# Deformable sampling, a scan and a mixture of experts in one kernel: a running sum over experts, interpolation on column groups, and half of the corner sum on GpSimd

## Chip, cores and metric

One core of a Trainium2 chip runs the program. The time is the device time of one execution in microseconds (us); three executions of the kernel before took 2467.89, 2460.09 and 2467.79, with a median of 2467.79 us.

## What is computed

For each of 16 images (64 channels, 128 x 128 pixels): bilinear samples of the image on a 32 x 32 grid give 1024 queries; a small network makes 8 sampling points of each query; bilinear samples there (four corners each) give keys and values; attention over the 8 points, with 8 heads, gives 1024 tokens. With 128 text tokens these 1152 tokens pass a linear recurrence over the batch and a mixture of 16 experts, of which each token uses two. Cut to what matters here:

```python
q_feat = bilinear_sample(feature_map, ref[:, :, None, :])[:, :, 0]
queries = q_feat @ W_q.T
h = jax.nn.gelu(layer_norm(q_feat @ W_o1 + b_o1, ln_g, ln_b))
off = (h @ W_o2 + b_o2).reshape(B, Nq, NHEAD, 2) * OFFSET_SCALE
sampled = bilinear_sample(feature_map, ref[:, :, None, :] + off * scale)
# bilinear_sample: v00*(1-wx)*(1-wy) + v01*wx*(1-wy) + v10*(1-wx)*wy + v11*wx*wy
...
hidden = jax.nn.silu(x @ w1[e]) * (x @ w2[e])        # for each of 16 experts e
out = sum over e of dispatch[:, e] * (hidden @ w3[e])  # dispatch is zero but for two experts
h = h + out
```

All of it is in float32.

## The kernel before

**Stages.** The kernel works through 16 images ("batches", index b). Per batch:

- `A1` (16 pieces): TensorE (PE) transposes the image from the load buffer `xin` (L712), ScalarE copies it to `pixmaj`, pixel rows with 64 channels (L843). SP stores `pixmaj` as a table in device memory.
- `A2` (8 pieces): PE interpolates the 32 x 32 grid, each of its 32 grid rows from two pixel rows (L727). The pixel row is the stationary operand (128 x 64), the interpolation matrix (32 columns) the moving one. ScalarE copies the result, 64 channels by 1024 queries, to `qfT` in two halves (L850).
- `B0`, `B1`: queries and the first layer of the offset network, 8 matmuls each (L735, L741), contraction over 64 partitions. `B1` to `B6` go on to the indices `idx` (L1142) and the corner weights `cw`. GpSimd takes the inverse square root in `B1` as a power (L585).
- `G` (32 pieces): GpSimd issues 64 gathers of 128 rows (L570), two a piece. Each row holds four corners. Behind each piece it clears a small tile `rest` (L577), `RESTS` = 2 times, waiting for each clearing to end.
- `D1` (j, f; 16 pieces): VectorE multiplies 512 KB of gathered rows by the corner weights into the one buffer `wsam` (L1062). `D2`: PE transposes the weighted rows and adds the four corners in PSUM as it does, 2 pairs x 4 corners (L690). ScalarE copies to `samT`; `D3`: PE computes keys and values (L700), ScalarE copies, VectorE multiplies by the query (L1068). `D5`, `S1` to `S3`: scores, softmax and the weighted sum of values on VectorE (L1072 to L1101).
- For each of three groups g of 384 tokens, `P1` to `P8`: layer norms (GpSimd takes their inverse square roots, L590), the recurrence, the gate, and the two best experts, which give `disp` (L1052).
- `X` (g, e; 48 pieces): PE computes both hidden products of one expert in three rotating banks `bank_h` (L624, L625); ScalarE applies silu (L780); VectorE multiplies into `hid` (L967), which holds all 16 experts.
- `W` (g, half, k; 18 pieces): for 128 tokens and 8 experts, PE multiplies `hid` (stationary, 128 x 128) by `w3` (moving, 64 columns) into `bank_o` (L634). ScalarE scales the eight results by `disp` in eight instructions (L831). `Z` on VectorE halves them in three additions (L975, L976) and `M2` adds both halves and the residual (L984, L985). SP stores the group.

A float32 matmul shows as two passes in the trace, each a weight load (PEld) and a product (PE); a transpose as one.

**What sets the order.** Nothing is scheduled when the program runs. For each engine's queue a string `ORDER` names the pieces in the order in which that engine does them, and every engine does its queue strictly in order. PE holds the pieces of three neighbouring batches interleaved with the experts: in the middle of the run PE's 48 `X` of a batch are mostly one or two pieces apart. `X(n)` waits for `hid(n-2)` and the silu of `n-1`, because it rewrites their banks. `W` waits for eight `hid`, and for the scaling of the last use of its bank. `D1` waits for its gathers and for the `D2` before (one `wsam`); a gather piece waits for the `D1` that last read its buffer (two buffers of 8 gathers). GpSimd's queue holds, per batch, 32 `G`, the power steps `P1`, `P5` (three each) and `B1`.

## Time and profile before

| | value |
|---|---|
| median of three runs | 2467.79 us |
| the profiled execution's own time | 2476.72 us |
| its span | 2474.9 us |
| PE busy | 2210.1 us, 89% |
| PE weight loads busy | 1979.4 us, 80% |
| VectorE busy | 1856.8 us, 75% |
| ScalarE busy | 1399.1 us, 57% |
| GpSimd busy | 1673.7 us, 68% |
| granted PE clock, mean share of full speed | 0.943 |

PE has the most work, and in the chain of waits that ended last it holds 58%, VectorE 11%, ScalarE 10%, GpSimd 8%, and 11% is "issue", time in which an engine waited for nothing that the profile shows. The shares are averages over a start in which the first image has to come in, a long middle in which one batch is like the next, and an end with experts only. Issuing instructions count as idle, so for GpSimd, which issues the gathers, the busy share leaves work out.

### The profile page before, as it was taken

The page shows a single profiled execution, that of the slowest core. Times are in us where ns is not written, and L with a number is a line of the kernel's source. Part 1 is how long each engine was busy: PE and PEld are TensorE (multiplying, and loading weights), DVE is VectorE, ACT ScalarE, POOL GpSimd, SP SyncE. Part 2 cuts the span into 40 slices and gives each one's busy share as a digit, 9 for nine tenths or more (in the row PEclk, how much of TensorE's full clock was granted, in tenths as well). Part 3 has the DMA queues.
Part 4 walks back from the last instruction along what each step waited for, and adds up shares of the span by engine and source line. Part 5 has one row for each costly group of instructions (what it writes and reads, how often), then busy time and mean ns, then how long its engine had stood idle before and what let it go on. Part 6 is the DMA issues. An engine that isn't in the chain of part 4 may idle for free.

```text
span 2474.9 us, 46859 instructions
## 1 busy us (share of the span) xinstructions
PE 2210.1 (89%) x15441; PEld 1979.4 (80%) x15441; DVE 1856.8 (75%) x4865; ACT 1399.1 (57%) x4344; POOL 1673.7 (68%) x2168
## 2 busy tenths in 40 slices
PE   2578989989999998999999899999999999989887
PEld 1566778888888888879889888888889888878776
DVE  1226888788788778888787878878787888887765
ACT  1124466566665656566565656656565666655555
POOL 0378887777686858868586877858686786867500
PEclk9967999999999999999899999989999999989989
DMA  9575636356472736538272745638173563712100
GB/s 221 148 207 154 182 104 186 113 164 173 110 217 66 213 97 177 167 106 222 77 212 85 198 138 152 186 95 225 52 221 108 166 175 109 201 52 68 49 3 6
DMA packets 362993, 346.85 MB, mean 140 GB/s; under 512 B 49152, under 2 KB 313472, under 8 KB 362624
## 3 DMA queue, kind: packets, MB, share of 16 engines
q1 hardware_dynamic: 313600, 209.57, 31.4%
q0 software_dynamic: 49152, 134.28, 18.6%
q8 instruction: 124, 2.03, 0.3%
q14 instruction: 117, 0.96, 0.1%
HBM read 205.87 MB, written 137.89 MB: 139 GB/s over the span
## 4 chain that ended last, share of the span: by engine, by line
PE 58%; issue 11%; DVE 11%; ACT 10%; POOL 8%; DMA 2%; ACTq 0%; DVEq 0%; another core or an unknown queue 0%; POOLq 0%
PE bank_o L634 16%; PE bank_h L624 8%; PE bank_d L700 7%; PE bank_h L625 7%; PE bank_d L690 7%; POOL gath L570 5%; ACT scaled L831 5%; PE bank_a L727 5%; PE bank_a L712 2%; POOL rest L577 2%; DMA gath<-table,idx 2%; DVE hid L967 2%; DVE wsam L1062 1%; PE bank_p L655 1%; PE bank_a L741 1%
## 5 line engine op out<-in xcount | busy, mean ns | idle before, releaser
L570 POOL DMA_INDIRECT gath<-table,idx x1024 | 1110.6, 1085 | 267.2 <-issue 238.5
L831 ACT ACTIVATE scaled<-bank_o,disp 128x64 f32<-128x64 f32 x2304 | 502.2, 330 | 370.8 <-PE bank_o L634 334.4
L624 PE MATMUL bank_h<-xsplit,w 128*128 128x384 f32 x1536 | 634.7, 413 | 83.3 <-ACT silu L780 52.9
L634 PEld LDWEIGHTS bank_o<-w_sb,hid 128*128 128x128 f32 x4608 | 567.9, 197 | 10.1 <-DVE hid L967 9.6
L634 PE MATMUL bank_o<-w_sb,hid 128*128 128x64 f32 x4608 | 563.8, 278 | 6.3 <-DVE hid L967 6.2
L625 PE MATMUL bank_h<-xsplit,w 128*128 128x384 f32 x1536 | 539.0, 351 | 0.0
L780 ACT ACTIVATE silu<-bank_h 128x384 f32<-128x384 f32 x768 | 393.8, 514 | 122.0 <-PE bank_h L625 104.2
L967 DVE TENSOR_TENSOR hid<-silu,bank_h 128x384 f32<-128x384 f32 x768 | 416.8, 548 | 53.4 <-ACT silu L780 38.5
L577 POOL MEMSET rest<- 1x400 f32 x1024 | 432.1, 422 | 29.6
L624 PEld LDWEIGHTS bank_h<-xsplit,w 128*128 128x128 f32 x1536 | 307.6, 200 | 139.5 <-ACT silu L780 68.0
L1062 DVE TENSOR_TENSOR wsam<-gath,cw 128x1024 f32<-128x1024 f32 x256 | 312.6, 1221 | 115.4 <-PE bank_d L690 54.7
L975 DVE TENSOR_TENSOR scaled<-scaled 128x256 f32<-128x256 f32 x576 | 205.8, 357 | 198.8 <-ACT scaled L831 165.5
L590 POOL TENSOR_TENSOR lns<-lns,neghalf 128x3 f32<-128x3 f32 x96 | 105.4, 1097 | 333.1 <-DVE lns L944 332.3
L690 PE MATMUL bank_d<-eye,wsam 128*128 128x128 f32 x2048 | 288.7, 287 | 37.5 <-DVE wsam L1062 33.2
L700 PE MATMUL bank_d<-w_kv,samT 128*128 128x256 f32 x1024 | 289.1, 406 | 29.9 <-ACT v_sb L817 17.4
L625 PEld LDWEIGHTS bank_h<-xsplit,w 128*128 128x128 f32 x1536 | 309.1, 201 | 4.7
L690 PEld LDWEIGHTS bank_d<-eye,wsam 128*128 128x128 f32 x2048 | 244.0, 149 | 55.8 <-DVE wsam L1062 44.1
L712 PE MATMUL bank_a<-eye,xin 128*128 128x128 f32 x1024 | 186.0, 312 | 80.4 <-DMA xin<-x_dram 39.0
L700 PEld LDWEIGHTS bank_d<-w_kv,samT 128*128 128x128 f32 x1024 | 183.4, 196 | 73.8 <-issue 39.3
L843 ACT COPY pixmaj<-bank_a 128x512 f32<-128x512 f32 x256 | 152.9, 597 | 154.8 <-PE bank_a L712 140.6
L712 PEld LDWEIGHTS bank_a<-eye,xin 128*128 128x128 f32 x1024 | 140.1, 161 | 116.6 <-issue 60.1
L813 ACT COPY k_sb<-bank_d 128x256 f32<-128x256 f32 x256 | 97.9, 382 | 166.9 <-PE bank_d L700 145.3
(141 smaller groups left out, 2306.2 us busy)
## 6 DMA issues: line engine op xcount, KB each, us to landing
table<-pixmaj SPq DMA_DIRECT2D x80, 1024.0 KB
xin<-x_dram SPq DMA_DIRECT2D x256, 256.0 KB
table<-pixmaj SPq DMA_DIRECT2D x32, 960.0 KB
table<-pixmaj SPq DMA_DIRECT2D x16, 1088.0 KB
gath<-table,idx POOLq DMA_INDIRECT x1024
out_dram<-ob SPq DMA_DIRECT2D x48, 96.0 KB
gath<-w_dram SPq DMA_DIRECT2D x4, 512.0 KB, 8.8
interp_sb<-interp_dram SPq DMA_DIRECT2D x1, 1024.0 KB, 5.3
```

The source lines that it names most:

```text
L570: pool.indirect_dma_start(out=gath[buf][:, p, :, :].rearrange("p a c -> p (a c)"), out_offset=None, in_=table[par], in_offset=bass.Indirec ...
L577: nc.gpsimd.memset(rest[:], 0.0).then_inc(rested, 1)
L624: mm(bank[:, 0:GC], w12[:, e, which, 0, :], xsplit[gp][:], start=True, stop=False)
L625: mm(bank[:, 0:GC], w12[:, e, which, 1, :], xsplit[gp][:], start=False, stop=True).then_inc(ready, 1)
L634: last = mm(bank_o[n % 2][:, C * i:C * (i + 1)], hid[:, e, 128 * k:128 * (k + 1)], w3_sb[:, e, :], start=True, stop=True)
L690: last = mm(bank_d[:, 128 * (2 * f + pair):128 * (2 * f + pair + 1)], wsam[:, corner, 2 * pair:2 * pair + 2, :].rearrange("p n c -> p (n c)"),
L700: last = mm(bank_d[:, 256 * i:256 * (i + 1)], samT[:, 2 * f + i, :], w_kv[:], start=True, stop=True)
L712: last = mm(bank_a[:, 128 * r:128 * (r + 1)], xin[u % 2][:, HW * (4 * (c % 2) + r):HW * (4 * (c % 2) + r + 1)], eye[:], start=True, stop=T ...
L780: nc.scalar.activation(silu[e % 2][:], bank_h[r][:, 0:GC], ACT.Silu).then_inc(silu_done, 1)
L831: last = nc.scalar.activation(scaled[n % 2][:, i, :], bank_o[n % 2][:, C * i:C * (i + 1)], ACT.Identity, scale=disp[gpar(par, g)][:, k, e: ...
L967: tt(hid[:, e, :], silu[e % 2][:], bank_h[r][:, 0:GC], ALU.mult).then_inc(hid_done, 1)
L1062: tt(wsam[:].rearrange("p a n c -> p n a c"), gath[j % GB][:, 4 * f:4 * f + 4, :, :], spread(w, 3, C), ALU.mult).then_inc(weighted, 1)
```

## The change

- The sum over experts becomes a running sum. `W` is now a piece per expert (48 a batch): three matmuls, one for each 128 tokens. ScalarE's part is gone. `Z` is now a piece per expert: three instructions of VectorE (scalar_tensor_tensor, 128 x 64) read `bank_o`, multiply by the token's `disp` and add the running sum in `ob`; the first expert adds the residual `h2` instead. Each waits for the one on the same tokens of the expert before. `M2`'s additions, `scaled` and `part` are gone. `hid` holds 4 experts (`HB`) for 16.
- The interpolation runs on column groups. The interpolation matrix (128 x 32) is now stationary, at one of four column positions, and the pixel row (64 columns) moves. The result stands with queries on partitions; a new piece `A3` transposes it (4 transposes, one more copy by ScalarE in place of one of the two). `B0` and `B1` now take two blocks of queries in one matmul, with block-diagonal weights `w_blk`: 4 matmuls each for 8.
- The corners are summed in two steps. A new piece `F` on GpSimd, two for each half `f` of a `j` (32 a batch), adds the far two corners to the near two (128 x 256 each); `D2` then has 2 pairs x 2 corners. `wsam` has two buffers. `RESTS` is 1.
- `ORDER` is new for every engine. `W(e)` stands behind `X(e+2)` on PE, `Z(e)` behind `hid(e+2)` on VectorE. On GpSimd the `F` pieces stand between the `G` pieces.

One batch of GpSimd's new queue, the middle one, read from the diff (G with its number, F with j, f and pair):

```
G0 G1 G2 G3 G4 G5 G6 P1 G7 F000 F001 F010 F011 G8 F100 G9 F101 G10 F110 G11 F111
P5 G12 F200 G13 F201 G14 F210 G15 F211 G16 F300 G17 F301 G18 P1 F310 G19 F311 G20
F400 F401 G21 F410 F411 G22 P5 F500 G23 F501 G24 G25 F510 G26 F511 G27 F600 G28
F601 G29 P1 F610 G30 F611 G31 B1 F700 F701 F710 F711 P5
```

The diff, without the order strings and the bookkeeping of semaphores:

```diff
-RESTS = 2
+RESTS = 1
+HB = 4
...
-        w_q = sb("w_q", [C, C])
-        w_off1 = sb("w_off1", [C, LH])
+        w_blk = sb("w_blk", [128, 2 * C + 2 * LH])
...
-        qfT = sb("qfT", [C, NQ])
+        qf_sb = sb("qf_sb", [128, QT * C])
+        qfT = sb("qfT", [128, QT // 2, 128])
...
-        wsam = sb("wsam", [128, 4, 4, C])
+        wsam = [sb(f"wsam{i}", [128, 4, 4, C]) for i in range(2)]
...
-        hid = sb("hid", [128, NE, GC])
-        scaled = [sb(f"scaled{i}", [128, 8, C]) for i in range(2)]
-        part = sb("part", [128, 2, GT, C])
+        hid = sb("hid", [128, HB, GC])
...
+        block_loads += [(w_blk[C * p:C * (p + 1), C * p:C * (p + 1)], wq) for p in range(2)]
+        block_loads += [(w_blk[C * p:C * (p + 1), 2 * C + LH * p:2 * C + LH * (p + 1)], w_o1) for p in range(2)]
...
-                wait(sp, ob_done, NGRP * b + g + 1)
+                wait(sp, eo_added, GT * NE * (NGRP * b + g + 1))
...
+                    elif kind == "F":
+                        j, f, pair = args
+                        pool.wait_ge(weighted, 16 * b + 2 * j + f + 1)
+                        near = wsam[f][:, 0:2, 2 * pair:2 * pair + 2, :].rearrange("p a n c -> p a (n c)")
+                        far = wsam[f][:, 2:4, 2 * pair:2 * pair + 2, :].rearrange("p a n c -> p a (n c)")
+                        nc.gpsimd.tensor_tensor(near, near, far, ALU.add).then_inc(folded, 1)
...
                     elif kind == "W":
-                        g, half, k = args
-                        n = 2 * GT * (NGRP * b + g) + GT * half + k
-                        pe.wait_ge(hid_done, SLOTS * b + NE * g + 8 * half + 8)
-                        wait(pe, eo_scaled, n - 1)
-                        for i in range(8):
-                            e = 8 * half + i
-                            last = mm(bank_o[n % 2][:, C * i:C * (i + 1)], hid[:, e, 128 * k:128 * (k + 1)],
+                        g, e = args
+                        n = SLOTS * b + NE * g + e
+                        pe.wait_ge(hid_done, n + 1)
+                        wait(pe, eo_added, GT * (n - 1))
+                        for k in range(GT):
+                            last = mm(bank_o[n % 2][:, C * k:C * (k + 1)], hid[:, n % HB, 128 * k:128 * (k + 1)],
                                       w3_sb[:, e, :], start=True, stop=True)
...
-                        pe.wait_ge(weighted, 16 * b + 2 * j + f + 1)
+                        pe.wait_ge(folded, 2 * (16 * b + 2 * j + f + 1))
...
-                            for corner in range(4):
+                            for corner in range(2):
 
                                 last = mm(bank_d[:, 128 * (2 * f + pair):128 * (2 * f + pair + 1)],
-                                          wsam[:, corner, 2 * pair:2 * pair + 2, :].rearrange("p n c -> p (n c)"),
-                                          eye[:], start=corner == 0, stop=corner == 3, is_transpose=True)
+                                          wsam[f][:, corner, 2 * pair:2 * pair + 2, :].rearrange("p n c -> p (n c)"),
+                                          eye[:], start=corner == 0, stop=corner == 1, is_transpose=True)
...
-                        if n == 4:
-                            pe.wait_ge(qf_stored, 2 * b + 1)
-                        for i in range(4 * n, 4 * n + 4):
-                            for r in range(2):
-                                row = FIRST_ROW[i] + r
-                                last = mm(bank_a[0:C, NG1 * (i % 16):NG1 * (i % 16 + 1)],
-                                          pixmaj[:, C * row:C * (row + 1)], interp_sb[:, i, r, :],
-                                          start=r == 0, stop=r == 1)
-                        if n % 4 == 3:
+                        for r in range(2):
+                            for a in range(4):
+                                row = FIRST_ROW[4 * n + a] + r
+                                last = mm(bank_a[NG1 * a:NG1 * (a + 1), C * n:C * (n + 1)], interp_sb[:, 4 * n + a, r, :],
+                                          pixmaj[:, C * row:C * (row + 1)], start=r == 0, stop=r == 1,
+                                          tile_position=(0, NG1 * a))
+                        if n == 7:
                             last.then_inc(qf_ready, 1)
+                    elif kind == "A3":
+                        pe.wait_ge(qf_stored, b + 1)
+                        for m in range(QT // 2):
+                            last = mm(bank_a[:, 128 * m:128 * (m + 1)], qf_sb[:, 128 * m:128 * (m + 1)], eye[:],
+                                      start=True, stop=True, is_transpose=True)
+                        last.then_inc(qfT_ready, 1)
...
                     elif kind == "B0":
-                        pe.wait_ge(qf_stored, 2 * b + 2)
-                        for t in range(QT):
-                            last = mm(bank_a[:, C * t:C * (t + 1)], qfT[:, 128 * t:128 * (t + 1)], w_q[:],
+                        pe.wait_ge(qfT_stored, b + 1)
+                        for m in range(QT // 2):
+                            last = mm(bank_a[:, 128 * m:128 * (m + 1)], qfT[:, m, :], w_blk[:, 0:2 * C],
                                       start=True, stop=True)
                         last.then_inc(q_ready, 1)
                     elif kind == "B1":
                         pe.wait_ge(q_stored, b + 1)
-                        for t in range(QT):
-                            last = mm(bank_a[:, LH * t:LH * (t + 1)], qfT[:, 128 * t:128 * (t + 1)], w_off1[:],
+                        for m in range(QT // 2):
+                            last = mm(bank_a[:, 2 * LH * m:2 * LH * (m + 1)], qfT[:, m, :], w_blk[:, 2 * C:2 * C + 2 * LH],
...
-                    elif kind == "W":
-                        g, half, k = args
-                        n = 2 * GT * (NGRP * b + g) + GT * half + k
-                        act.wait_ge(eo_ready, n + 1)
-                        act.wait_ge(disp_done, NGRP * b + g + 1)
-                        wait(act, pair_sum, n - 1)
-                        for i in range(8):
-                            e = 8 * half + i
-                            last = nc.scalar.activation(scaled[n % 2][:, i, :], bank_o[n % 2][:, C * i:C * (i + 1)],
-                                                        ACT.Identity, scale=disp[gpar(par, g)][:, k, e:e + 1])
-                        last.then_inc(eo_scaled, 1)
...
-                    elif kind == "A2" and args[0] % 4 == 3:
-                        half = args[0] // 4
-                        if half == 0 and b == 0:
+                    elif kind == "A2":
+                        if b == 0:
                             setup()
-                        act.wait_ge(qf_ready, 2 * b + half + 1)
+                        act.wait_ge(qf_ready, b + 1)
+                        wait(act, qfT_ready, b)
+                        copy(qf_sb[:], bank_a[:]).then_inc(qf_stored, 1)
+                    elif kind == "A3":
+                        act.wait_ge(qfT_ready, b + 1)
                         wait(act, off1_ready, b)
-                        copy(qfT[:, 512 * half:512 * (half + 1)], bank_a[0:C, :]).then_inc(qf_stored, 1)
+                        copy(qfT[:].rearrange("p a b -> p (a b)"), bank_a[:]).then_inc(qfT_stored, 1)
...
-                        if e % 8 == 0:
-
-                            wait(dve, eo_ready, 2 * GT * (NGRP * b + g - 1) + GT * (e // 8 + 1))
+                        wait(dve, eo_ready, n - HB + 1)
                         r = (2 * (NE * g + e) + 1) % 3
-                        tt(hid[:, e, :], silu[e % 2][:], bank_h[r][:, 0:GC], ALU.mult).then_inc(hid_done, 1)
+                        tt(hid[:, n % HB, :], silu[e % 2][:], bank_h[r][:, 0:GC], ALU.mult).then_inc(hid_done, 1)
                     elif kind == "Z":
-                        g, half, k = args
-                        n = 2 * GT * (NGRP * b + g) + GT * half + k
-                        sums.start(n)
-                        dve.wait_ge(eo_scaled, n + 1)
-                        eo = scaled[n % 2]
-                        for m in (4, 2):
-                            link(sums, tt(eo[:, 0:m, :], eo[:, 0:m, :], eo[:, m:2 * m, :], ALU.add))
-                        tt(part[:, half, k, :], eo[:, 0, :], eo[:, 1, :], ALU.add).then_inc(pair_sum, 1)
-                    elif kind == "M2":
-                        g = args[0]
+                        g, e = args
                         gp = gpar(par, g)
-                        mix.start(NGRP * b + g)
-                        dve.wait_ge(pair_sum, 2 * GT * (NGRP * b + g + 1))
-
-                        wait(dve, out_done[gp], 8 * NGRP * b + 8 * (g - gp))
-                        link(mix, tt(ob[gp][:], part[:, 0, :, :], part[:, 1, :, :], ALU.add))
-                        tt(ob[gp][:], ob[gp][:], h2[g][:], ALU.add).then_inc(ob_done, 1)
+                        n = SLOTS * b + NE * g + e
+                        dve.wait_ge(eo_ready, n + 1)
+                        if e == 0:
+                            wait(dve, out_done[gp], 8 * NGRP * b + 8 * (g - gp))
+                        for k in range(GT):
+                            if e:
+                                dve.wait_ge(eo_added, GT * (n - 1) + k + 1)
+                            stt(ob[gp][:, k, :], bank_o[n % 2][:, C * k:C * (k + 1)], disp[gp][:, k, e:e + 1],
+                                (ob[gp] if e else h2[g])[:, k, :], ALU.mult, ALU.add).then_inc(eo_added, 1)
...
-                        wait(dve, sam_ready, 16 * b + 2 * j + f)
+                        wait(dve, sam_ready, 16 * b + 2 * j + f - 1)
                         w = cw[par][:, HEADS * j + 4 * f:HEADS * j + 4 * f + 4, :]
-                        tt(wsam[:].rearrange("p a n c -> p n a c"), gath[j % GB][:, 4 * f:4 * f + 4, :, :],
+                        tt(wsam[f][:].rearrange("p a n c -> p n a c"), gath[j % GB][:, 4 * f:4 * f + 4, :, :],
```

## Rows read from the trace of the kernel before

**Rows 1.** The window 500 to 2000 us: length; busy (x) of PE, PEld, DVE, ACT, POOL; PEclk, DMA, GB/s
```profile
500.00:2000.00 1500.00, 1409.12 (x10117) 1275.29 (x10117) 1213.53 (x3186) 921.27 (x2871) 1112.13 (x1434) 0.96 0.55 152
```

**Rows 2.** Timeline, VectorE: `idx` (L1142) of batches 3 and 15, start and duration
```profile
499.45 0.23 DVE L1142 SCALAR_TENSOR_TENSOR idx<-xyf 128x64 int32<-128x64 f32 x1
...
2203.99 0.23 DVE L1142 SCALAR_TENSOR_TENSOR idx<-xyf 128x64 int32<-128x64 f32 x1
```

**Rows 3.** What POOL waits for in 500 to 2000 us: total, times, longest
```profile
POOL lns L590 <- DVE lns L944: 186.2, 37, 17.7
POOL gath L570 <- issue: 158.0, 669, 0.4
```

**Rows 4.** ScalarE and VectorE groups of the expert sum, whole run: busy, mean ns, idle before
```profile
L831 ACT ACTIVATE scaled<-bank_o,disp 128x64 f32<-128x64 f32 x2304 | 502.2, 330 | 370.8 <-PE bank_o L634 334.4
...
L975 DVE TENSOR_TENSOR scaled<-scaled 128x256 f32<-128x256 f32 x288 | 121.6, 422 | 188.9 <-ACT scaled L831 165.5 <-issue 19.4 <-DVE disp L1052 2.8
L975 DVE TENSOR_TENSOR scaled<-scaled 128x128 f32<-128x128 f32 x288 | 84.2, 292 | 9.9
L976 DVE TENSOR_TENSOR part<-scaled 128x64 f32<-128x64 f32 x288 | 65.0, 226 | 9.8
```

**Rows 5.** Timeline, VectorE: one piece `Z`, then two small steps of `P8`
```profile
1306.21 0.74 DVE L975 TENSOR_TENSOR scaled<-scaled 128x256 f32<-128x256 f32 x2
1306.98 0.22 DVE L976 TENSOR_TENSOR part<-scaled 128x64 f32<-128x64 f32 x1
1307.13 0.55 DVE L967 TENSOR_TENSOR hid<-silu,bank_h 128x384 f32<-128x384 f32 x1
...
1316.93 0.21 DVE L1050 TENSOR_TENSOR disp<-disp,top_p 128x48 f32<-128x48 f32 x1
1317.06 0.20 DVE L1051 TENSOR_TENSOR pick<-pick,top_p 128x48 f32<-128x48 f32 x1
```

**Rows 6.** Window 500 to 2000 us, PE and PEld busy: L690, L727, L735, L741 in order
```profile
500.00:2000.00 1500.00, 182.26 (x1344) 155.37 (x1344) 0.96 0.55 152
500.00:2000.00 1500.00, 87.98 (x1280) 80.19 (x1280) 0.96 0.55 152
500.00:2000.00 1500.00, 19.95 (x160) 18.57 (x160) 0.96 0.55 152
500.00:2000.00 1500.00, 20.31 (x160) 19.31 (x160) 0.96 0.55 152
```

**Rows 7.** Chain of waits from 1301 us: start, duration, engine and line
```profile
1301.52 0.17 PE bank_h L624
1301.86 1.73 PE bank_o L634 x16
1303.59 0.23 PE bank_h L624
...
1309.55 0.88 PE bank_d L690 x8
```

**Rows 8.** GpSimd groups by shape in 500 to 2000 us, then a setup clearing
```profile
L570 POOL DMA_INDIRECT gath<-table,idx x681 | 739.5, 1086 | 176.6 <-issue 158.0 <-DVE idx L1142 18.4 <-DVE wsam L1062 0.2
L577 POOL MEMSET rest<- 1x400 f32 x680 | 287.0, 422 | 19.6
L590 POOL TENSOR_TENSOR lns<-lns,neghalf 128x3 f32<-128x3 f32 x63 | 71.0, 1127 | 186.7 <-DVE lns L944 186.2
...
L554 POOL MEMSET w_kv<- 128x256 f32 x1 | 0.3, 316 | 0.0
```

**Rows 9.** Timeline: a gather beside a two-input VectorE instruction; durations (min/median/max) of all gathers
```profile
1434.02 2.23 DVE L1090 TENSOR_TENSOR v_sb<-v_sb,score 128x2048 f32<-128x2048 f32 x1
1434.36 2.72 POOL L570 DMA_INDIRECT gath<-table,idx  x1 [0.30 <-issue]
...
L570 POOL DMA_INDIRECT gath<-table,idx x1024: 942/959/3055, 102.6 to 2329.4; - x171
```

**Rows 10.** Groups, whole run: the passes of `W`, busy and mean duration
```profile
L634 PE MATMUL bank_o<-w_sb,hid 128*128 128x64 f32 x4608 | 563.8, 278 | 6.3 <-DVE hid L967 6.2
```

205 lines of the change are left out of this document (108 added, 97 removed), and 8 rows, old and new, of the table KINDS.

## Prediction

> **What bounds the kernel now.** I read the busy table first, then a long stretch in the middle, because one batch is repeated 16 times and only the first three and the last run differently. From 500 to 2000 us PE is busy 1409 of 1500 us, VectorE 1214, GpSimd 1112, ScalarE 921 [rows 1]. The indices of batch 3 are ready at 499.45 us and those of batch 15 at 2203.99 us [rows 2], so a batch takes 1704.5 / 12 = 142.05 us. Multiplying row 1 by 142.05 / 1500 = 0.0947 gives the work of one batch: PE 133.4, VectorE 114.9, ScalarE 87.2, GpSimd 105.3 us. PE is idle for 8.6 us of a batch, and it is the bound.
>
> The reader should not stop at GpSimd's 105.3. Between its gathers the profile shows 158.0 us of "issue", 15.0 a batch, that is not counted as busy and can hold nothing else [rows 3]. GpSimd's own work is therefore 120.3 us a batch; what is left is mostly waiting for layer norm variances (186.2 us in the window, 17.6 a batch). So three engines stand at 133, 120 and 115 of 142. A change that takes work from PE and gives some to the other two can gain only until the next of them is full.
>
> **The expert sum.** ScalarE loses its 2304 scalings, 502.2 us of the run, 31.4 a batch [rows 4]. It was not the bound; the gain is that a silu no longer queues behind eight of them. VectorE loses 18 pieces `Z` a batch. One lasts from 1306.21 to the next start at 1307.13, 0.92 us [rows 5]: 16.6 us. It also loses `M2`: two additions of 192 columns, which by the slope between 128 and 256 columns (292 and 422 ns, 1.02 ns a column [rows 4]) are 0.36 us each, three times a batch: 2.1 us. It gains 48 x 3 = 144 multiply-adds of 64 columns. Neither a 64-column step on PSUM with a scalar per partition nor its spacing is in the trace. Below: two steps of 48 columns that don't depend on each other start 0.13 us apart [rows 5]. Above: if each must end before the next, it is 226 ns [rows 4] plus the 0.03 us gap of the dependent steps in `Z` [rows 5], 0.256. Each of the 144 waits on the sum three instructions back, never on its neighbour, so I take the near end with 16 more columns, rounded up: 0.16 us, 23.0 us a batch (18.7 to 36.9). VectorE: 114.9 - 16.6 - 2.1 + 23.0 = 119.2.
>
> PE keeps the same 288 passes a batch of `W` (144 matmuls, two passes each), but in 48 pieces for 18. The first step of an `X` holds the chain 0.23 us behind a `W` and 0.17 behind another `X` [rows 7]: 30 x 0.06 = +1.8 us. `W(e)` stands behind `X(e+2)` in the new order, whose own wait already asks for `hid(e)`, so it adds no wait of its own for that. It also waits for `Z(e-2)`, which VectorE does right behind `hid(e)`, 0.48 us later, while `X(e+2)` holds PE for 0.7 (four steps of 0.17 [rows 7]); hidden, unless other VectorE work lies between. `hid(n)` needs `W(n-4)`, long past. SP's output now waits for the last `Z`; its store stands at no one's head.
>
> **Corners.** `D2` goes from 128 transposes a batch to 64. Removed are 64 passes: 0.110 us each in the chain (0.88 / 8 [rows 7]) or 0.136 by busy time (182.26 / 1344 [rows 6]), so 7.0 to 8.7; I take 8.0. The second `wsam` lets `D1` start earlier, worth nothing while VectorE isn't the bound.
>
> **Interpolation.** `B0` and `B1` were 160 passes each in the window, 19.95 and 20.31 us [rows 6], 3.8 a batch, and are halved: -1.9. The new `A3` is four transposes: +0.45. `A2` keeps 128 passes, 87.98 us or 8.3 a batch, 0.065 each [rows 6]. Its weights shrink from 64 to 32 columns and its moving side grows from 32 to 64. Below: half of now, 4.2, if the weights set the pace and the four column groups run together. Above: a pass of `W` with the same 64 moving columns under 128 columns of weights, 1.73 / 16 = 0.108 [rows 7], 13.8. I stay near the present kind, at 7.3: -1.0. Where the row shows one `W` pass lasting 278 ns at a spacing of 108 [rows 7, 10], an emptied array would cost 0.17 us more; the new order has 103 runs of `A2`, 12.9 changes of form a batch, 2.2 us.
> The Trainium skill, TensorEngine Tiling (Array Packing), Key Properties, says that changing the tiling mode drains TensorE. By that rule those 2.2 us would be added to PE's sum; no row of before has a tiled matmul.
>
> PE: 133.4 + 1.8 - 8.0 - 1.9 + 0.45 - 1.0 = 124.8 us. With its present 8.6 of idle time it would allow 133.4 a batch.
>
> **GpSimd.** One clearing of two goes: 0.422 us and 0.029 of gap (19.6 / 680) [rows 8], 32 x 0.451 = -14.4. In its place 32 additions of two 256-column operands. Below: a clearing of 256 columns, 0.316 us, which reads nothing. Above: the power step, 1.127 us on 3 columns [rows 8], a heavier function. An add is nearer the clearing in kind but moves three streams for one, so I take twice it: 0.65.
> The Trainium skill, GPSIMD Engine Reference, Performance versus the Vector engine, gives 4497 ns for such an add of 2048 elements; an eighth is 0.56, an estimate, and with it the forecast would be some 35 us lower.
>
> That is not all. The gather that starts at 1434.36 lasts 2.72 us, to within a microsecond of the end of a 2.23 us VectorE instruction that reads two SBUF operands; the shortest takes 0.942 [rows 9], the mean 1.086 [rows 8]. So a GpSimd instruction loses 0.14 us on average to VectorE. I give each addition 0.15: 0.80 in all, 25.6 a batch. The same collision may hold two-input VectorE steps, for which no row has a price: from nothing to the whole of every addition, 32 x 0.65 = 21 us. If VectorE lost per addition what a gather loses, it would be 4.6; GpSimd lost rather than shared in that row, so I take about half, 2.5: VectorE 121.7.
>
> GpSimd: 120.3 - 14.4 + 25.6 = 131.5 us, now the fullest. Moved into its in-order queue are waits: each `F` waits for `D1`, and the later gathers and the power steps wait behind it. The order issues two to three gather pieces (4 to 6 gathers) after the last one that an `F` needs, but one at `F(5,0)` and none at `F(7,1)`; the latter stands where GpSimd waits for indices anyway. For this I add 6 us, less than PE's 8.6 because GpSimd has those gathers in hand: 137.5 us a batch.
>
> **The sum.** 12 batches x (137.5 - 142.05) = -55. The first batches follow GpSimd alone: +32 x 0.35 = +11. After the last index PE and ScalarE set the pace with fewer steps: -9. Together -53 on the profiled execution's own 2476.7 us: 2424. That execution was 8.9 above the median of the runs, so I predict 2415 us.
>
> **Rivals.**
> (B) The addition is cheap. At 0.316 + 0.15 GpSimd needs 120.8 and PE is again the bound at 133.4: 12 x -8.7 = -104, +1, -12, so 2353. For it: nothing in the trace shows an arithmetic GpSimd step without the power function.
> (C) GpSimd's queue becomes a bound worse than PE is now. It decides on F, the addition with what holds it, at its place behind each `D1`: 120.3 - 14.4 + 32 F + 6 passes 142.05 at F = 0.94 us. At 1.0 it is 143.9 a batch: +22, +18, -8, so 2500; with the power step's price far above. For it: the 2.72 us gather. Against: the clearing's 0.316.
> Ours lies between B and C, on one number. The Trainium skill, SBUF — State Buffer, SBUF: two separate sides, says the shared pair of ports is locked for a whole instruction and the loser fully blocks. The trace agrees with its 2.72 us gather; what a reading GpSimd step does to VectorE no row of before shows.
> (D) The running sum is serial: 0.256 a step makes VectorE 135.6, with its waits about 144.3 a batch, 2495. Against: the waits reach three steps back.
> (E) The column groups give nothing and drain the array: `A2` at 13.8 and 2.2 more put PE at 133.5, with 8.6 idle 142: 2465, no change. This is the tiling rule at full price.
>
> **Numbers.** Ours 0.47, B 0.22, C 0.19, D 0.04, E 0.08. About 0.3% is what a measurement of this kernel tells from no change. Faster is ours and B less the edge of ours, 0.68; the same 0.09; slower 0.23. The range takes in B's end and C's first step: 2340 to 2500.
>
> **What would show it.** The addition's mean near 0.8 us with VectorE steps beside the long ones; GpSimd busy near 120 a batch with little left but issue; L634 unchanged in passes, L690 halved; multiply-adds 0.16 apart; a period of 137 to 138. An addition over 0.94 or a period set by waits of GpSimd for `wsam` makes it wrong upwards; one near 0.4 with PE at 94% again, downwards.

## The result, and the profile after

The changed kernel takes 2514.46 us, the median of 4 runs (2511.19 to 2525.84). Four runs of the kernel before beside it gave 2466.61. The ratio is 1.0208, with a 95% interval of 1.0171 to 1.0245: slower by 48 us, where 2415 us had been forecast, and outside the range of 2340 to 2500. The profiled execution took 2514.73 us. One kernel further down, the kernel before with one clearing, had two of its four runs in a slower state (2839.01 and 3242.29 us), so beside its median of 2828.59 stand its two fast runs, 2790.00 and 2818.18 us.

The busy table of the page:

```profile
PE 2068.7 (82%) x14225; PEld 1826.0 (73%) x14225; DVE 2167.8 (86%) x6209; ACT 955.1 (38%) x2040; POOL 1871.3 (74%) x2169
```

The window from 500 to 2000 us, with the columns of [rows 1]:

```profile
500.00:2000.00 1500.00, 1284.64 (x9080) 1144.40 (x9079) 1380.68 (x3972) 611.12 (x1305) 1201.63 (x1379) 0.92 0.52 147
```

VectorE's timeline has the indices of batches 3 and 15, as in [rows 2]:

```profile
508.04 0.22 DVE L1146 SCALAR_TENSOR_TENSOR idx<-xyf 128x64 int32<-128x64 f32 x1
...
2269.28 0.22 DVE L1146 SCALAR_TENSOR_TENSOR idx<-xyf 128x64 int32<-128x64 f32 x1
```

A batch takes 1761.2 / 12 = 146.8 us, where it took 142.05. The spans differ by 38.0 us: +8.6 up to batch 3, +56.7 in the twelve periods, -27.3 after the last indices. The window times 146.8 / 1500 gives PE 125.7 us a batch, VectorE 135.1, ScalarE 59.8 and GpSimd 117.6. PE's granted clock is 0.92 there for 0.96, but PE is idle for 21 us of a batch. All that GpSimd waits for in the window, to set against [rows 3] (total, times, longest):

```profile
POOL gath L581 <- issue: 150.2, 636, 0.4
POOL wsam L599 <- DVE wsam L1066: 65.9, 31, 4.7
POOL lns L607 <- DVE lns L956: 53.2, 22, 5.4
POOL gath L581 <- DVE idx L1146: 28.9, 11, 3.1
POOL off_s L602 <- DVE off_s L1117: 1.3, 1, 1.3
```

With the issue time GpSimd's queue holds 132.3 us of work a batch, and waits for 14.6. VectorE at 92% looks like the bound and GpSimd at 80% busy does not. The chain of waits that ended last, where PE held 58% before, now goes through both:

```profile
DVE 35%; POOL 23%; PE 19%; issue 8%; DMA 2%; ACT 0%; DVEq 0%
```

GpSimd's groups by shape in the window [rows 8]:

```profile
L581 POOL DMA_INDIRECT gath<-table,idx x656 | 737.0, 1123 | 180.5 <-issue 150.2 <-DVE idx L1146 28.9
L599 POOL TENSOR_TENSOR wsam<-wsam 128x256 f32<-128x256 f32 x323 | 257.5, 805 | 66.5 <-DVE wsam L1066 65.9
L588 POOL MEMSET rest<- 1x400 f32 x328 | 138.4, 422 | 0.1
```

The addition by itself, whole run: durations (min/median/max), first and last start:

```profile
L599 POOL TENSOR_TENSOR wsam<-wsam x512: 711/722/2492, 102.5 to 2408.4; 128x256 f32<-128x256 f32 x171
```

VectorE's groups of the whole run; the first is the new multiply-add. Steps that the change did not touch got longer: the products of `k_sb` had a mean of 421 ns before and have 524 now; a step of three numbers had 230 and has 421:

```profile
L988 DVE SCALAR_TENSOR_TENSOR ob<-bank_o,disp,ob 128x64 f32<-128x64 f32 x2160 | 476.3, 278 | 25.7 <-PE bank_o L650 24.8
...
L1072 DVE TENSOR_TENSOR k_sb<-k_sb,q_sb 128x256 f32<-128x256 f32 x256 | 134.0, 524 | 61.1 <-ACT v_sb L837 60.9
...
L956 DVE TENSOR_SCALAR lns<-lns 128x3 f32<-128x3 f32 x96 | 40.4, 421 | 3.3
```

The timeline (start, duration, engine, line) shows how. The VectorE product that took 1.22 us before (its median) lasts 2.67 beside two additions that take 1.40 together:

```profile
1322.05 2.67 DVE L1066 TENSOR_TENSOR wsam<-gath,cw 128x1024 f32<-128x1024 f32 x1 [0.81 <-DMA gath<-table,idx]
1322.23 1.40 POOL L599 TENSOR_TENSOR wsam<-wsam 128x256 f32<-128x256 f32 x2
...
1326.49 2.34 DVE L954 TENSOR_TENSOR lnsq<-lnx 128x192 f32<-128x192 f32 x1
1327.21 1.41 POOL L599 TENSOR_TENSOR wsam<-wsam 128x256 f32<-128x256 f32 x2
```

The mean of each unchanged step after, less its mean before, times its count, adds up to 178 us of the run, 11.1 a batch. The same kernel without the additions, the first of the experiments, stands at 124.0 us of VectorE's work a batch, 11.1 less. The Trainium skill, SBUF — State Buffer, SBUF: two separate sides, says that the loser of the shared ports fully blocks. These lines agree: 1.22 and the 1.40 of the additions make 2.62 of the 2.67. The same section gives the ports to whichever starts first; by the timeline both VectorE steps had started first and were the ones held. Mostly it is VectorE that loses, in steps of three numbers too; an addition loses 0.08 us on average (0.799 mean, 0.722 median).

### The profile page after: what moved, and what is told of

The parts are those of the page before. It is cut to its first block, busy times and chain, and to the rows that moved or that the text cites. A ratio compares the mean times of both kernels' runs of the same rounds, so it can differ in the third digit from the quotient of the medians.

```text
span 2512.9 us, 44418 instructions
## 1 busy us (share of the span) xinstructions
PE 2068.7 (82%) x14225; PEld 1826.0 (73%) x14225; DVE 2167.8 (86%) x6209; ACT 955.1 (38%) x2040; POOL 1871.3 (74%) x2169
## 4 chain that ended last, share of the span: by engine, by line
DVE 35%; POOL 23%; PE 19%; issue 8%; DMA 2%; ACT 0%; DVEq 0%
POOL gath L581 14%; DVE ob L988 6%; POOL wsam L599 6%; PE bank_o L650 6%; PE bank_h L641 4%; DVE hid L977 4%; DVE v_sb L1101 3%; PE bank_h L642 3%; DVE wsam L1066 3%; DVE v_sb L1094 2%; POOL rest L588 2%; DMA gath<-table,idx 2%; PE bank_d L716 2%; DVE k_sb L1072 2%; DVE score L1076 1%
## 5 line engine op out<-in xcount | busy, mean ns | idle before, releaser
L581 POOL DMA_INDIRECT gath<-table,idx x1024 | 1138.7, 1112 | 278.9 <-issue 233.8
L650 PEld LDWEIGHTS bank_o<-w_sb,hid 128*128 128x128 f32 x4608 | 660.9, 206 | 117.9 <-issue 101.2
L641 PE MATMUL bank_h<-xsplit,w 128*128 128x384 f32 x1536 | 639.2, 416 | 119.1 <-DVE hid L977 117.7
L650 PE MATMUL bank_o<-w_sb,hid 128*128 128x64 f32 x4608 | 656.9, 282 | 72.3 <-DVE ob L988 68.9
L642 PE MATMUL bank_h<-xsplit,w 128*128 128x384 f32 x1536 | 554.4, 361 | 0.0
L988 DVE SCALAR_TENSOR_TENSOR ob<-bank_o,disp,ob 128x64 f32<-128x64 f32 x2160 | 476.3, 278 | 25.7 <-PE bank_o L650 24.8
L599 POOL TENSOR_TENSOR wsam<-wsam 128x256 f32<-128x256 f32 x512 | 405.5, 799 | 104.0 <-DVE wsam L1066 103.4
L641 PEld LDWEIGHTS bank_h<-xsplit,w 128*128 128x128 f32 x1536 | 317.8, 207 | 164.6 <-DVE hid L977 121.1
L642 PEld LDWEIGHTS bank_h<-xsplit,w 128*128 128x128 f32 x1536 | 320.3, 209 | 2.5
L706 PE MATMUL bank_d<-eye,wsam 128*128 128x128 f32 x1024 | 172.3, 297 | 64.2 <-POOL wsam L599 61.9
L588 POOL MEMSET rest<- 1x400 f32 x512 | 216.0, 422 | 0.2
L728 PEld LDWEIGHTS bank_a<-eye,xin 128*128 128x128 f32 x1024 | 134.9, 161 | 96.8 <-issue 43.9
L706 PEld LDWEIGHTS bank_d<-eye,wsam 128*128 128x128 f32 x1024 | 130.5, 157 | 87.5 <-POOL wsam L599 77.7
```

The source lines that it names most:

```text
L581: pool.indirect_dma_start(out=gath[buf][:, p, :, :].rearrange("p a c -> p (a c)"), out_offset=None, in_=table[par], in_offset=bass.Indirec ...
L599: nc.gpsimd.tensor_tensor(near, near, far, ALU.add).then_inc(folded, 1)
L641: mm(bank[:, 0:GC], w12[:, e, which, 0, :], xsplit[gp][:], start=True, stop=False)
L642: mm(bank[:, 0:GC], w12[:, e, which, 1, :], xsplit[gp][:], start=False, stop=True).then_inc(ready, 1)
L650: last = mm(bank_o[n % 2][:, C * k:C * (k + 1)], hid[:, n % HB, 128 * k:128 * (k + 1)], w3_sb[:, e, :], start=True, stop=True)
L706: last = mm(bank_d[:, 128 * (2 * f + pair):128 * (2 * f + pair + 1)], wsam[f][:, corner, 2 * pair:2 * pair + 2, :].rearrange("p n c -> p ( ...
```

## The experiments

First account (theory 1): the additions hold VectorE, and its 92% sets the period. Rival (theory 2): GpSimd's in-order queue sets it. All ratios are to the kernel before on the same chip, with the 95% interval. Differences in us go across chips, on which the kernel before took 2463.40 to 2473.08 us.

**Without the additions.** PE sums all four corners again and both clearings are back; running sum, column groups, orders and the two `wsam` stay.

```diff
-RESTS = 1
+RESTS = 2
-                        nc.gpsimd.tensor_tensor(near, near, far, ALU.add).then_inc(folded, 1)
+                        pass
-                            for corner in range(2):
+                            for corner in range(4):
```

> The changed kernel with GpSimd's additions undone: TensorE sums four corners again, GpSimd clears twice behind each gather piece; orders, running sum and column groups stay. In the changed kernel VectorE is busy 135.1 us of a 146.8 us batch, 11.1 of it because steps that the kernel before also has last longer. Theory 1, the additions hold VectorE: its work falls to about 124, TensorE's rises by 8 to about 134 with idle time 138 to 141, and the time is 2390 to 2440. Theory 2, GpSimd's queue (132.3 us of work and 14.5 of waits) set the period: about the same 2390 to 2440, since this run takes both away. Theory 3, the running sum per expert, with TensorE waiting for each hid and each bank, set it: 2480 or more, near the changed kernel.

2351.56 us, ratio 0.9515 (0.9484 to 0.9546), faster than expected. The rest of the change gains 121 us by our own median of before, 2473.08, and the exchange of a clearing for an addition costs 163 (2514.46 less 2351.56), or 171 by the two ratios. Both theories had named the same range, so this doesn't tell them apart.

**A clearing in place of the addition**, at the same place with the same waits.

```diff
-                        nc.gpsimd.tensor_tensor(near, near, far, ALU.add).then_inc(folded, 1)
+                        wait(pool, folded, 4 * (8 * b + j) + 2 * f + pair)
+                        nc.gpsimd.memset(rest2[:], 0.0).then_inc(folded, 1)   # rest2: [1, 750]
```

> The changed kernel with each of GpSimd's additions replaced by a clearing of about the same length (750 elements of one partition, about 0.71 us by the slope of the clearings), at the same place, with the same wait before it and the same signal after it. It reads nothing. The far two corners are left out of the sum. Theory 1 (the additions hold VectorE's steps): lnsq, k_sb and the small norm steps go back to their lengths before, VectorE falls from 135.1 to 124 a batch, and the time falls by 11 times 16 or so, to 2330 to 2420. Theory 2 (GpSimd's queue and its waits): GpSimd has as much to do as before, the time stays within 0.5% of the changed kernel's 2514. Theory 3 (running sum): it stays too.

2406.61 us, 0.9744 (0.9706 to 0.9781). I took this for the hold of VectorE. It was no clean test: the clearing lasts 717 ns and is never held, so GpSimd's own work fell too, from 132.3 to 129.1 us a batch.

**One clearing, without additions**: the first of these kernels with `RESTS = 1`. **And the kernel before with `RESTS = 1`.**

```diff
-RESTS = 2
+RESTS = 1
```

> The run without the additions, but with one clearing behind each gather piece for two, so GpSimd has 106 us of work a batch. Theory 1: as without the additions and two clearings, within 10 us, because GpSimd is not the bound. Theory 2: faster than that run by up to 7 us a batch, 50 to 100 us in all, as long as GpSimd's queue is what the others wait for.

> The kernel before with one clearing behind each gather piece for two. It prices the clearing that the change removed. TensorE is the bound there (133.4 of 142.05 us), so by every theory within 8 us of 2467; if gathers that come closer together disturb something (landing, VectorE), it is slower by 10 us or more.

2547.84 us, 1.0314 (1.0276 to 1.0351), and 2828.59 us, 1.1436 (1.1371 to 1.15), or 1.13 by the 2790.00 and 2818.18 named above. Both theories failed badly in the first kernel, and in the second what had been named as the other possibility happened: taking work from GpSimd cost 196 and 330 to 356 us. In the second one's timeline all engines pause behind "remote" and "issue", that is, for nothing that the profile shows, while GpSimd issues a gather every 1.4 us:

```profile
1316.26 0.95 POOL L570 DMA_INDIRECT gath<-table,idx  x1 [0.30 <-issue]
1317.20 0.42 POOL L577 MEMSET rest<- 1x400 f32 x1
1317.79 0.95 POOL L570 DMA_INDIRECT gath<-table,idx  x1 [0.16 <-issue]
...
1319.50 0.58 ACT L850 COPY qfT<-bank_a 64x512 f32<-64x512 f32 x1 [3.19 <-remote]
...
1320.49 0.55 DVE L967 TENSOR_TENSOR hid<-silu,bank_h 128x384 f32<-128x384 f32 x1 [3.60 <-remote]
1320.51 0.19 PEld L624 LDWEIGHTS bank_h<-xsplit,w 128*128 128x128 f32 x1 [1.31 <-issue]
```

Over the run ScalarE and VectorE wait 257 and 149 us behind "remote", 2.9 and 2.0 before. Of the two DMA queues that the page calls "instruction", this kernel delivered nothing from 1310 to 1323 us, while the kernel before had a packet on each. That is little to go by: the kernel before has a stretch as long with none, from 1363 to 1376 us. I read it as engines that run out of instructions while gathers come too close. That reading is inferred, and no run tests it; the time is shown.

**One long clearing** and **one of 650**, in the kernel before.

```diff
-RESTS = 2
+RESTS = 1
-        rest = sb("rest", [1, 400])
+        rest = sb("rest", [1, 930])   # and [1, 650]
```

> The kernel before with one clearing behind each pair of gathers as in the run that lost 14%, but of 930 elements, about as long (0.87 us) as the two of 400. Theory 1 (what counts is the time between the gathers, in which other traffic, the engines' own instructions among it, gets through): 2473 us within 10, and no idle time of the engines with nothing that they waited for beyond that of the kernel before. Rival (the number of instructions between the gathers counts, or the pairing of waits): 2600 to 2830 us.

> The kernel before with one clearing of 650 elements (about 0.63 us) behind each pair of gathers, between the 0.42 us that cost 14% and the 0.87 us that cost nothing. Theory 1 (there is a rate of gathers up to which nothing is lost, as the changed kernel with 0.42 us and an addition suggests): 2470 us within 15. Rival (the loss grows steadily with the rate): 2580 to 2680 us.

2468.18 us, 1.0012 (0.9996 to 1.0028), and 2622.25 us, 1.0608 (1.0536 to 1.068). So it is time that counts and not the number of clearings: behind a pair of gathers 0.42 us costs 13 to 14%, 0.63 costs 6%, 0.87 nothing. That nothing would be lost at 0.63 was wrong; where between 0.63 and 0.87 the loss begins was not measured.

**The parts alone, on the kernel before**: the running sum, and the column groups with `A3` and the block-diagonal `B0` and `B1`. Each is the change's own hunk with an order of its own; of the first this is the core, of the second the other:

```diff
+                            stt(ob[gp][:, k, :], bank_o[n % 2][:, C * k:C * (k + 1)], disp[gp][:, k, e:e + 1],
+                                (ob[gp] if e else h2[g])[:, k, :], ALU.mult, ALU.add).then_inc(eo_added, 1)
...
+    ("A3", "pe"): [()],
+    ("A3", "act"): [()],
```

> The kernel before with the running sum alone: W, Z and hid as in the change, the corners in four transposes, two clearings, the interpolation as before. Theory 1 (the gain of the kernel without additions came from work taken from PE by the column groups, since PE at 94% set the period): PE keeps its 133 us a batch and gets 1.8 more, VectorE rises to about 124 a batch by 144 multiply-adds of 0.195 us; no gain, 2470 to 2500 us. Theory 2 (the gain came from the expert sum, because ScalarE no longer scales 2304 pieces and its silus come on time): most of the 121 us, 2370 to 2400 us.

> The kernel before with the interpolation on column groups alone (A2 in four column groups, A3, block-diagonal B0 and B1), everything else as before. Theory 1 (PE's work sets the period): PE falls from 133.4 to about 127.5 a batch, 8.3 to 3.65 in A2, 1.9 in B0 and B1, 0.45 more for A3; 12 x -6.1 and somewhat more in the last batches: 2375 to 2410 us. Theory 2 (the expert sum made the gain): a small part of it, 2440 to 2465 us. If neither alone comes near 121 us and both together do, the two engines PE and ScalarE or VectorE were bounds in turn.

2434.71 us, 0.9872 (0.9824 to 0.9921), and 2419.95 us, 0.9813 (0.9788 to 0.9839). Neither theory is right alone: 31 and 46 us. The kernel without the additions, with both, gains 121; it also has the second `wsam` and the new orders, and no run tells their share from that of the two parts together. The column kernel's PE load fell to 127.5 us a batch, as worked out, but the period only to 138.7.

**ScalarE scales again, one VectorE addition per expert**, without and then with the corner additions.

```diff
+                        for k in range(GT):
+                            last = nc.scalar.activation(scaled[n % 2][:, k, :], bank_o[n % 2][:, C * k:C * (k + 1)],
+                                                        ACT.Identity, scale=disp[gpar(par, g)][:, k, e:e + 1])
...
-                        for k in range(GT):
-                            stt(ob[gp][:, k, :], bank_o[n % 2][:, C * k:C * (k + 1)], disp[gp][:, k, e:e + 1],
+                        tt(ob[gp][:], scaled[n % 2][:], (ob[gp] if e else h2[g])[:], ALU.add).then_inc(eo_added, 1)
```

> The kernel without additions (all four corners by PE, two clearings), and ScalarE scales the three results of an expert, after which VectorE adds them to the sum in one instruction of 192 columns in place of three multiply-adds: 48 x 0.36 = 17.3 us a batch for 144 x 0.195 = 28.1, and ScalarE's 31 us back. Theory 1 (in the kernel without additions VectorE, at 91%, holds the period together with PE): VectorE falls from 124 to about 114 a batch, 2310 to 2340 us. Rival (PE's 126 us and its waits on ScalarE hold it; silus queue behind the scalings again): 2350 to 2390 us.

> The changed kernel, its additions and one clearing kept, with ScalarE scaling the three results of an expert and VectorE adding them in one instruction of 192 columns. VectorE's load falls from 135.1 us a batch by about 28 - 17 = 11 to 124, GpSimd's stays 132.3, PE's 125.7. Theory 1 (VectorE at 92% sets the changed kernel's period; relieved of 11 us, GpSimd with its 132.3 and some waits sets it, 137 to 140 a batch): 2400 to 2440 us. Rival (the loss comes from GpSimd's queue or from PE's waits for the folded corners): above 2490 us. And against the kernel that scales with ScalarE and has no additions (2336 us) it says what the additions alone cost where VectorE has room.

2336.11 us, 0.9473 (0.9449 to 0.9498): VectorE's load fell from 124.0 to 110.2 a batch, 11%, and the time by 15 us, 0.6%, so VectorE had hardly been the bound. With the additions 2512.64 us, 1.0199 (1.0158 to 1.0241), where theory 1 gave 2400 to 2440. Theory 1 alone fails here by 70 us. It is not shown that VectorE's load counts for nothing: it fell by 6.4 us a batch where 11 had been worked out. The window shows VectorE 56 us lighter than the changed kernel's, and GpSimd as it was:

```profile
500.00:2000.00 1500.00, 1286.16 (x9106) 1148.27 (x9105) 1324.80 (x2993) 930.25 (x2790) 1194.65 (x1385) 0.92 0.53 148
```

**Seven more clearings**, and **each addition in two halves**, in the changed kernel.

```diff
+                for _ in range(2 if k < 7 else 1):     # gathers 0 to 6 of a batch have no addition behind them
...
-                        nc.gpsimd.tensor_tensor(near, near, far, ALU.add).then_inc(folded, 1)
+                        for a in range(2):
+                            nc.gpsimd.tensor_tensor(near[:, a, :], near[:, a, :], far[:, a, :], ALU.add).then_inc(folded, 1)
```

> The changed kernel with the second clearing back behind the first seven pieces of gathers of a batch, the ones that no addition follows, and only there. Theory 1 (in the changed kernel the additions keep the gathers apart and its loss is all VectorE's hold): 7 x 0.45 us more for GpSimd, which doesn't set the period; 2512 within 10 us. Rival (part of the loss is the dense gathers of these seven pieces, in which the engines go without their instructions as they do with one clearing throughout): 2460 to 2495 us.

> The changed kernel with each addition of 128x256 written as two of 128x128, one behind the other. Theory 1 (a VectorE step is held for what is left of a whole GpSimd instruction, so halves hold half as long and let VectorE in between): the additions' holds fall from 11.1 us a batch to 6 or 8, GpSimd gets 2 to 4 us more: 2470 to 2500 us. Rival (what is lost is in proportion to the bytes that GpSimd moves, or VectorE loses again to the second half): 2505 to 2540 us.

2557.59 us, 1.0378 (1.0327 to 1.043), and 2552.98 us, 1.0367 (1.0321 to 1.0413). The first was to be free or a gain, and cost 43 us: GpSimd's work rises by 2.6 us a batch and the period by 3.2, so clearings that compute nothing on an engine 80% busy are paid for in full. The second is past its rival's range too: a half takes 548 ns on average, and GpSimd's work rises to 137.1 a batch.

That gave a third account (theory 3): the load of GpSimd's queue sets the period, waits and all (the expectations of the first two runs call something else by that number). Four kernels tried it: the clearing in the addition's place at 970 elements; the addition on a scratch tile that nobody waits for; no clearing where an addition follows and two elsewhere (24 a batch for 32); and that with ScalarE's scaling.

```diff
-        rest2 = sb("rest2", [1, 750])
+        rest2 = sb("rest2", [1, 970])
...
+                        nc.gpsimd.tensor_tensor(scr[:, 0], scr[:, 0], scr[:, 1], ALU.add).then_inc(folded, 1)
...
+                        gather_points(b, par, args[0], 0 if todo[i + 1][0] == "F" else 2)
```

> The kernel that clears a scratch row where the changed one adds (the two far corners are left out of the sum), with the clearing at 970 elements, about 0.90 us, for 750 and 0.717 us: GpSimd's load goes from 126.6 to about 132.5 us a batch, the changed kernel's, with no instruction that moves two operands. Theory 3 (the load of GpSimd's in-order queue sets the period, one for one): 2406 + 12 x 5.9 = 2477 us, at most 2500. Theory 1 (the additions' hold on the other engines is what costs): 2406 us within 12.

> The changed kernel with its additions at the same places and of the same size, but on a scratch tile: they wait for nothing of VectorE's and nobody waits for them; PE sums all four corners, as in the kernel without additions. GpSimd's load is 120.8 - 14.4 + 25.6 = 132 us, PE's 126. If load and holds make the loss, 2480 to 2515 us; if it is the waits between the engines that the addition makes (for D1 before it, PE for the folded corners behind it), 2370 to 2440 us.

> The changed kernel, additions kept, with clearings only behind gathers that no addition follows, two there, and none where one follows: 24 clearings a batch for 32, 3.6 us less for GpSimd; the gathers stay 0.8 us or more apart. Theory 3 (GpSimd's load sets the period): 12 to 16 x -3.6, so 2455 to 2475 us. Theory 1 (the addition's hold): 2512 within 10. Rival (0.8 us between the gathers is too little; one clearing of 0.63 us in the kernel before cost 6%): above 2530 us.

> The same placing of the clearings with ScalarE scaling the experts' results, so with 11 us a batch less on VectorE and 3.6 less on GpSimd. Theory 3: GpSimd alone counts, so as a2_spaced within 15 us (2450 to 2475). Rival (VectorE and GpSimd bound each other in turn through the waits, and relieving one alone is not seen): 2400 to 2440 us.

In order: 2474.05 us, 1.0043 (1.0018 to 1.0067); 2539.08, 1.0313 (1.0268 to 1.0358); 2482.51, 1.0092 (1.0059 to 1.0125); 2439.55, 0.9918 (0.989 to 0.9946). The first is the clean test that the 750-element clearing was not: against the 750-element kernel only the clearing's length differs, 0.18 us more each, and 67 us are lost (74 by the two ratios) where 71 had been worked out. In the chain of waits that ended last of that kernel GpSimd holds 65%. GpSimd's groups in the window of that kernel:

```profile
L582 POOL DMA_INDIRECT gath<-table,idx x666 | 747.1, 1122 | 183.4 <-issue 121.8 <-POOL rest L599 32.5 <-DVE idx L1146 29.1
L599 POOL MEMSET rest<- 1x970 f32 x328 | 295.0, 899 | 33.3 <-DVE wsam L1066 24.6
L589 POOL MEMSET rest<- 1x400 f32 x332 | 140.2, 422 | 0.1
```

and all its engines in that window:

```profile
500.00:2000.00 1500.00, 1293.09 (x9147) 1150.85 (x9146) 1294.88 (x3998) 614.00 (x1312) 1243.81 (x1398) 0.93 0.53 149
```

In this group a gather's wait behind GpSimd's own clearing (32.5) is GpSimd's work and not a wait for others; with it the work is 135.0 us a batch, and the waits for other engines are 9.2. The changed kernel has less work, 132.3, more waits, 14.6, and takes 40 us more. So a full queue by itself explains a kernel that is no faster than before (1.0043). The rest of the way to 1.0208 comes with the additions as such.

The second takes the waits of the addition away and is 25 us slower, above both its ranges: its mean addition lasts 855 ns, GpSimd's load is 134.2 and not 132, PE's four corners put it at 130.2, and GpSimd waits for layer norm variances instead (107.5 us of the window). So taking away the waits for `D1` alone gains nothing. The third gains 32 us, less than expected; the fourth 75, inside the rival's range. Between these two only VectorE's and ScalarE's part differs, and it is worth 43 us: GpSimd's work stays (130.4 and 129.9) and its waits fall from 13.7 to 10.9. So VectorE does count through GpSimd's waits.

**Less load in the fastest kernel**: one clearing of 750 behind a pair, or one of 320 behind each gather.

The second one's edit (the first has `RESTS = 1` and 750 elements in the code as it was):

```diff
-        rest = sb("rest", [1, 400])
+        rest = sb("rest", [1, 320])
                     ).then_inc(gath_in[buf][p // 4], 16)
-                for n in range(RESTS * (4 * QT * b + k), RESTS * (4 * QT * b + k + 1)):
+                    n = RESTS * (4 * QT * b + k) + p % 2
                     wait(pool, rested, n)
                     nc.gpsimd.memset(rest[:], 0.0).then_inc(rested, 1)
```

> The kernel without additions and with ScalarE's scaling, its two clearings of 400 elements behind each pair of gathers (0.87 us) replaced by one of 750 (0.72 us): 32 x 0.156 = 5.0 us a batch less for GpSimd. Theory 3 (GpSimd's load sets the period down to PE's 124 us and its waits): 12 to 16 x -5.0, so 2255 to 2276 us. Theory 4 (a pair of gathers needs nearly 0.87 us behind it; in the kernel before 0.63 us cost 6% and 0.42 us 14%): slower than 2336 us, 2350 to 2420.

> As v4_one_clearing_750, but with a clearing of 320 elements (0.355 us) behind each single gather: the same sum, evenly placed. Theory 4a (the mean rate of gathers counts): as v4_one_clearing_750 within 10 us. Theory 4b (two gathers close together are what shuts the others out, so even spacing needs less of it): at least 30 us faster than v4_one_clearing_750, and at best 2255 to 2276 us.

2291.29 us, 0.9292 (0.9258 to 0.9326), and 2270.68 us, 0.9202 (0.9169 to 0.9235). Lighter queues gain, 45 and 65 us, and neither has pauses beyond those of the kernel with two clearings, so theory 4 falls for 0.72 us in this kernel. But theory 3 had given the first 2255 to 2276: GpSimd's work falls by 4.4 us a batch and the period by 2.2 only, with PE at 94%. Even spacing is worth 21 us, between the bounds of 4a and 4b; the issue time before a gather shrinks with it (118.4 us in the window for 169.8). This last kernel is the fastest of all, and PE is its bound again, at 95%:

```profile
500.00:2000.00 1500.00, 1423.46 (x10904) 1314.43 (x10906) 1262.57 (x3297) 1027.82 (x3099) 1145.89 (x1547) 0.96 0.58 163
```

GpSimd's gathers and clearings in that window:

```profile
L586 POOL DMA_INDIRECT gath<-table,idx x734 | 803.3, 1094 | 148.7 <-issue 118.4 <-DVE idx L1155 28.6 <-DVE wsam L1075 1.6
L593 POOL MEMSET rest<- 1x320 f32 x733 | 260.2, 355 | 0.1
```

The kernels side by side, in us a batch; GpSimd's work includes issue and its waits behind its own clearings, and all is from the window times the period, as above:

| kernel | period | PE | VectorE | GpSimd's work | GpSimd waits |
|---|---|---|---|---|---|
| before | 142.05 | 133.4 | 114.9 | 120.3 | 20.0 |
| changed | 146.8 | 125.7 | 135.1 | 132.3 | 14.6 |
| without additions | 136.1 | 126.2 | 124.0 | 120.8 | 13.4 |
| clearing 750 for it | 139.9 | 123.9 | 124.1 | 129.1 | 10.0 |
| clearing 970 for it | 144.9 | 124.9 | 125.1 | 135.0 | 9.2 |
| addition nobody waits for | 148.9 | 130.2 | 135.8 | 134.2 | 14.1 |
| seven more clearings | 150.0 | 128.3 | 134.0 | 134.9 | 14.2 |
| addition in two | 148.4 | 126.2 | 132.1 | 137.1 | 11.2 |
| eight clearings fewer | 145.4 | 126.1 | 131.4 | 130.4 | 13.7 |
| the same, ScalarE scales | 142.1 | 123.7 | 122.7 | 129.9 | 10.9 |
| additions, ScalarE scales | 145.7 | 124.9 | 128.7 | 130.7 | 14.8 |
| no additions, ScalarE scales | 134.6 | 124.1 | 110.2 | 121.0 | 11.7 |
| this, 750 behind each pair | 132.4 | 124.6 | 111.5 | 116.6 | 15.8 |
| this, 320 behind each gather | 131.7 | 125.0 | 110.8 | 111.0 | 20.7 |
| before, one long clearing | 140.2 | 131.7 | 116.0 | 120.6 | 20.3 |
| before, running sum alone | 140.7 | 132.1 | 125.8 | 120.5 | 18.4 |
| before, column groups alone | 138.7 | 127.5 | 114.4 | 121.0 | 15.2 |

That work and waits add up to about the period is true of any engine. The finding is in the last two columns. In the nine kernels in which GpSimd has more than 125 us of work, 9 to 15 us of waits stay, however full its queue is. When the clearing alone is lengthened (750 to 970), work rises by 5.9, waits fall by 0.8 and the period rises by 5.0: it follows the work. Kernels with additions have 10.9 to 14.8 us of waits, those with a clearing in their place 9.2 and 10.0. Where PE's work is 94 or 95% of the period, GpSimd's waits grow to 16 to 21. The kernels with too short a clearing are left out; GpSimd waits there for 38 to 60 us.

The pauses behind "remote" and "issue" differ from kernel to kernel too. ScalarE, VectorE and PE have 95 us of them in the window before and 1.3 with the one long clearing, and both take the same time, so at this size they cost nothing that can be told. The changed kernel has 3.8 us, its variants up to 156, the kernel before with one clearing of 0.42 us 544.

## Why the prediction was wrong

The step that failed is "For this I add 6 us, less than PE's 8.6 because GpSimd has those gathers in hand: 137.5 us a batch". GpSimd's own work was forecast at 131.5 and is 132.3. But its waits are 14.6: 6.5 for `D1`, 5.2 for variances, 2.8 for indices (the rows above times 146.8 / 1500). 131.5 + 14.6 is 146.1, the measured period but for 0.7. In the kernel with the 970-element clearing, whose queue is at least as full, 9.2 us of waits stay, and it comes out about even (1.0043). The other 5.4 of the 14.6 us come only with the additions, which hold VectorE for 11.1 us a batch where 2.5 stood. That they come by way of VectorE is likely, since a lighter VectorE took waits off in one pair of kernels (13.7 to 10.9), but in the other pair it did not (14.6 and 14.8), and so it stays open. I had read the 17.6 us for variances [rows 3] as slack that a fuller queue would use up. It used only a part: the indices and variances of a batch come out of a chain that passes through this same queue, and an in-order queue can't move later gathers ahead of them. That last sentence is argued from the order, not shown; that 9 to 15 us stay is shown.

GpSimd's work was forecast rightly, its idle time was not, and with it the sign. With 14.6 us of waits the addition would have had to take under 0.67 us to reach 142.05, less than its shortest, 0.711.

Term by term:
- Addition, 0.80 forecast: 0.799 mean over the run. Right in the sum, with luck in the parts: undisturbed 0.72 where 0.65 stood, and held for 0.08 where 0.15 stood.
- PE, 124.8 forecast, 125.7 measured, but by terms that cancel. `A2` costs 36.51 us of the window for 1280 passes, 3.6 a batch, where 7.3 stood. `D2` costs 104.57 for 648 passes, 10.2 a batch for 17.3: -7.0 and not -8.0, at a granted clock of 0.92 for 0.96. Against them the passes of `W` rose from 34.9 to 40.8 a batch (416.5 us of the window for 368.5), 5.9 where 1.8 stood. Its wait for `Z`, taken as hidden, is 44.2 us of the window, 4.3 a batch, on an engine that has the time. No cost of draining shows in `A2`'s busy time, and the column kernel gained; rival E is out.

```profile
500.00:2000.00 1500.00, 36.51 (x1280) 23.76 (x1280) 0.92 0.52 147
...
500.00:2000.00 1500.00, 104.57 (x648) 79.20 (x648) 0.92 0.52 147
```

- Multiply-adds, 0.16 apart forecast: three last 0.66 by the timeline, the first alone 0.27, so 0.195 apart, 28.1 us a batch for 23.0.

```profile
1306.57 0.66 DVE L988 SCALAR_TENSOR_TENSOR ob<-bank_o,disp,ob 128x64 f32<-128x64 f32 x3
```

- What the additions cost VectorE, 2.5 forecast, 11.1 measured, inside the bounds of 0 to 21. VectorE came out at 135.1 for 121.7. Taking work off VectorE and keeping the additions gained nothing that can be told in the changed kernel, 2512.64 for 2514.46, and 43 us in the one with eight clearings fewer.
- First batches, +11 forecast, +8.6. After the last index -9 forecast, -27.3, three times what I gave; no run says which of the fewer steps does it.
- A clearing was priced as 0.451 us of GpSimd and nothing else. In the changed kernel that held: seven clearings put back only cost time. As a price of the clearing it was wrong: in the kernel before, the time it fills is needed.

Of the rivals, C gave the right end (2500) and the right engine, but made it hang on an addition of over 0.94 us; at 0.80 it happened by the waits. B's cheap addition did not come, and D's serial sum was too dear at 0.256 a step.

## What to carry to other kernels

When work moves to an engine whose queue runs in order and feeds a chain, forecast the period as its work plus waits. The waits that it has now are the upper end, and take off only those for which you can say which chain gets shorter. Here 20.0 us of waits became 14.6 (9.2 with a load that computes nothing), and 6 had been forecast. Try the load by itself with an instruction that computes nothing before moving real work. And an instruction that computes nothing is not free to remove: it may be spacing out the gathers, as it did here.

## What the runs showed of the hardware that I had not expected

- Gathers issued by GpSimd two at a time with 0.42 us behind them make the whole kernel slower: 1.13 to 1.14 times the time, and 1.0608 at 0.63 us; 1.0012 at 0.87. In the kernel without additions and with ScalarE's scaling, going from 0.87 to 0.72 us gained 45 us.
- VectorE steps of three numbers are held by GpSimd's additions as long ones are: 230 ns to 421 on average, and 300 in the same kernel without the additions. A step of 1.22 us took 2.67 beside two additions though it had started first.
- A pass of 32 columns of weights in four column groups costs 0.029 us of PE's busy time at a granted clock of 0.92, where the same pass with 64 weight columns and half the moving side cost 0.069 at 0.96 [rows 6].
